# Folding q's second layer into k's in a linear-attention and soft-MoE block on one Trainium2 core

## The reference

```python
def _mlp(x, W1, b1, W2, b2):
    h = jax.nn.gelu(x @ W1 + b1, approximate=False)
    return h @ W2 + b2
q = _mlp(x, W1q, b1q, W2q, b2q)
k = _mlp(x, W1k, b1k, W2k, b2k)
v = _mlp(x, W1v, b1v, W2v, b2v)
scores = jnp.einsum('bid,bjd->bij', q, k) / scale
scores = scores * mask
out = jnp.einsum('bij,bjd->bid', scores, v)
...
x = _layernorm(x + attention, axis=-1)
x = _layernorm(x + soft_moe(x), axis=-1)
```

## Time and profile before

| what | value |
|---|---|
| median of 3 runs | 684.1 us (683.0 to 685.0) |
| the profiled execution: its time, its span | 684.8 us, 683.1 us |
| mean granted TensorE clock | 0.982 |
| PE busy | 643.4 us (94% of the span), 4032 matmuls |
| PEld busy | 581.2 us |
| DVE busy | 446.1 us (65%) |
| ACT busy | 441.2 us (65%) |
| POOL busy | 301.9 us (44%) |

### The profile page before, as it was taken

The page is one execution under the profiler, slowest core; times in us unless marked ns, Lnnn a source line. Parts: engine busy times, 40 slices in busy tenths (PEclk is TensorE's granted clock), DMA queues, the critical chain, the costliest instruction groups (busy, mean ns, idle before and its releaser), DMA issues. The chain is left out here.

```text
span 683.1 us, 12110 instructions
## 1 busy us (share of the span) xinstructions
PE 643.4 (94%) x4032; PEld 581.2 (85%) x4032; DVE 446.1 (65%) x912; ACT 441.2 (65%) x910; POOL 301.9 (44%) x325
## 2 busy tenths in 40 slices
PE   5899999999999999999999999965999999979994
PEld 4789899888898998998988989955999999967883
DVE  5457677677677775776767767776555555345884
ACT  4655767767767668677677676645666666524775
POOL 2433654745536447446365374324433333202443
PEclk9989999999999999999999999996999999999998
DMA  7201201112102011020120100003000000030444
GB/s 240 62 32 32 61 5 60 32 32 62 31 31 61 11 50 34 28 61 31 31 61 31 31 32 1 1 0 63 0 1 0 0 0 1 1 62 31 155 154 154
DMA packets 29299, 30.19 MB, mean 44 GB/s; under 512 B 5298, under 2 KB 25172, under 8 KB 29268
## 3 DMA queue, kind: packets, MB, share of 16 engines
q1 hardware_dynamic: 29248, 29.78, 14.4%
q10 hardware_dynamic: 20, 0.01, 0.0%
HBM read 21.39 MB, written 8.39 MB: 44 GB/s over the span
## 5 line engine op out<-in xcount | busy, mean ns | idle before, releaser
L419 POOL TENSOR_TENSOR v_lo<-xn_all,v_hi 128x512 fp32r<-128x512 f32 x32 | 41.3, 1291 | 114.1 <-ACT v_hi L494 114.1
L476 ACT ACTIVATE h_hi<-bank,bias_col 128x512 fp32r<-128x512 f32 x96 | 66.3, 691 | 31.1 <-PE bank L580 29.0
L856 DVE TENSOR_TENSOR state_lo<-bank,state_hi 128x512 fp32r<-128x512 f32 x58 | 40.0, 690 | 61.6 <-ACT state_hi L509 61.6
L578 PE MATMUL bank<-xnT_hi,w_hi 128*128 128x512 f32 x192 | 77.3, 403 | 1.6 <-DVE xnT_lo L810 1.6
L579 PE MATMUL bank<-xnT_lo,w_hi 128*128 128x512 f32 x192 | 77.2, 402 | 0.0
L580 PE MATMUL bank<-xnT_hi,w_lo 128*128 128x512 f32 x192 | 77.0, 401 | 0.0
L1256 PE MATMUL bank<-xn_all,e_tok 128*128 128x257 f32 x256 | 66.4, 382 | 0.1
L816 DVE TENSOR_TENSOR h_lo<-bank,h_hi 128x512 fp32r<-128x512 f32 x64 | 44.1, 689 | 34.1 <-ACT bank L478 34.1
L1167 ACT ACTIVATE e_tok<-bank,shift,xinv 128x256 f32<-128x256 f32 x64 | 36.1, 564 | 42.6 <-PE bank L1241 21.8
L1336 DVE COPY ET_all<-bank 128x256 f32 (+1 forms) x64 | 27.1, 424 | 55.1 <-PE bank L1250 54.9
L413 POOL TENSOR_TENSOR h_lo<-xn_all,h_hi 128x512 fp32r<-128x512 f32 x32 | 41.4, 1294 | 35.6 <-ACT xn_all L478 33.8
(11 more groups left out here) (168 smaller groups left out, 2118.3 us busy)
## 6 DMA issues: line engine op xcount, KB each, us to landing
xn_all<-in_xT SPq DMA_DIRECT2D x16, 512.0 KB, 3.7
x_all<-in_L_attn_x SPq DMA_DIRECT2D x16, 512.0 KB, 3.5
out<-xn_all SPq DMA_DIRECT2D x16, 512.0 KB, 3.0
w_sb<-in_L_ffn_w SPq DMA_DIRECT2D x2, 512.0 KB, 5.2
xn_all<-in_L_ffn_w SPq DMA_DIRECT2D x2, 512.0 KB, 6.4
x_all<-in_L_attn_W1k SPq DMA_DIRECT2D x1, 256.0 KB, 4.2
x_all<-in_L_attn_W1q SPq DMA_DIRECT2D x1, 256.0 KB, 4.6
x_all<-in_L_attn_W1v SPq DMA_DIRECT2D x1, 256.0 KB, 4.8
```

Source lines behind the costliest of these rows:

```text
L419: pool.tensor_tensor(v_lo[:, pair, :], v_tok[:, pair, :], v_hi[:, pair, :].bitcast(F32), ALU.subtract).then_inc(v_split, 1)
L476: nc.scalar.activation(h_hi[:, n, m, :], ps, ACT.Gelu, bias=bias(n, m))
L578: nc.tensor.matmul(ps, w[0], xs[0], start=start, stop=False, skip_group_check=shared)
L856: nc.vector.tensor_tensor(lo[:, :, :], state_halves, hi[:, :, :].bitcast(F32), ALU.subtract).then_inc(state_split, 1)
```

## The change

The product q . k is rewritten. With hq and hk the gelu outputs, q = hq W2q + b2q and k = hk W2k + b2k, so q . k = hq . (W2q k) + b2q . k. The kernel therefore computes once M = W2k W2q^T (`fold_weights`, 258 columns: 256 of the product and two equal ones, W2k b2q) and for each tile k' = hk M + a constant row (`project_k`, token-major, 128x258). q's second layer is gone; scores and state use hq itself. Column 256 of k' is gamma_j = b2q . k_j, one number per key. It enters the scores as a number added before the mask (`mask_scores`, now four operations, one for each chunk), and for all earlier chunks as the running sum of gamma_j v_j, which is the same row for all later queries: `carry` adds gamma times v of this chunk, with gamma's column as a broadcast weight, to the output tile of the next chunk, and ACT's `preload` copies that tile on to the one after. The scores of a group move from the end of its own body to the next body, behind the first hidden job; all four chunks come later in a body. k' is now in token-major form at first, so k's rounding for the state reads SBUF and its subtraction moves from DVE to POOL (`split_ktok`), and the transposed copy goes through ACT and DVE (`round_kT`, `split_kT`). Six column loads of b2q and b2k (128 elements of 4 bytes each) are new.

```diff
-            HK, HQ, HV, K2, Q2, V2, KT = (0, 1), (2, 3), (4, 5), (6, 7), (8, 9), (10, 13), (11, 12)
...
+            HK, HQ, HV, K2, V2, KT = (0, 1), (2, 3), (4, 5), (6, 7, 8, 9), (10, 12), (11, 13)
...
                     a = g - 1
                     if project:
                         add_ln_b(g)
+                        split_hv(g, 0)
                     if attend:
                         invert_o(a, 0)
                     if project:
-                        split_hv(g, 0)
                         split_hv(g, 1)
                         if more:
                             split_x(g + 1)
+                        split_ktok(g, 0)
                     if attend:
                         invert_o(a, 1)
                     if project:
+                        split_ktok(g, 1)
...
+                for kb in range(KB):
+                    for col in (D, D + 1):
+                        act.dma_start(w2q_in[:, kb, col:col + 1], b2q[kb * P:(kb + 1) * P].rearrange(
+                            "(p o) -> p o", o=1)).then_inc(fold_loaded, 16)
...
+                def round_ktok(g):
+
+                    if not (isinstance(g, int) and g == 0):
+                        act.wait_ge(chunk_done, GT * g)
+                    act.wait_ge(k_biased, GT * g + GT)
+                    nc.scalar.copy(gam_hi[:, :], k_tok[:, :, D]).then_inc(gam_rounded, 1)
+                    for m in range(2):
+                        pair = slice(2 * m, 2 * m + 2)
+                        nc.scalar.copy(ktok_hi[:, pair, :], k_tok[:, pair, 0:D]).then_inc(ktok_rounded, 1)
+
+                def round_kT(g, j, m):
+                    act.wait_ge(kT_done, KB * g + m + 1)
+                    nc.scalar.copy(k_hi[:, m, :], job_bank(j, KT[m])[:, :]).then_inc(kT_rounded, 1)
+
+                def preload(ba, i):
+
+                    act.wait_ge(carried, CB * ba + i - 1)
+                    act.wait_ge(z_ready, TB * ba + i + 2 - i % 2)
+                    nc.scalar.copy(out_tile(i % GT), out_tile((i - 1) % GT)).then_inc(preloaded, 1)
...
+                    def follow(c):
+                        i = GT * ja + c
+                        if i + 1 < TB:
+                            round_state(ba, i + 1)
+                        if i + 2 < TB:
+                            preload(ba, i + 2)
+
...
-                        round_state(ba, GT * ja + 3)
-                    round_k(g, j, 0)
-                    round_k(g, j, 1)
-                    if attend and ja < GB - 1:
-                        round_state(ba, GT * ja + 4)
-                    round_q(g, j, 0)
-                    round_q(g, j, 1)
+                        follow(2)
+                        if settle:
+                            apply_z(act, a - 1, (ja - 1) % 2, range(GT))
+                        follow(3)
+                    round_ktok(g)
+                    round_kT(g, j, 0)
                     round_v(g, 0)
-                    round_ktok(g, j, 0)
-                    if attend and settle:
-                        apply_z(act, a - 1, (ja - 1) % 2, (1, 2, 3))
...
+                def fold_weights():
+
+                    pe.wait_ge(fold_loaded, 16 * 8)
+                    for half in range(KB):
+                        for kb in range(KB):
+                            last = nc.tensor.matmul(out_ps[half][:, 0:KC], w2k_in[:, kb, half * P:(half + 1) * P],
+                                                    w2q_in[:, kb, :], start=(kb == 0), stop=(kb == KB - 1))
+                    last.then_inc(m_done, 1)
...
+                def mark_out():
+
+                    pe.wait_ge(m_split, KB)
+                    for ps in out_ps:
+                        last = nc.tensor.matmul(ps[:, :], ident[:, :], causal[:, :, :].rearrange("p c n -> p (c n)"),
+                                                start=True, stop=True)
...
+                def project_k(g, j, t):
+                    if t < 2:
+                        pe.wait_ge(hkq_split, 4 * g + t + 3)
+                    else:
...
+                        last = split3(job_bank(j, K2[t])[:, 0:KC], (h_hi[:, K_SLOT, kb, toks], h_lo[:, K_SLOT, kb, toks]),
+                                      (m_hi[:, kb, :], m_lo[:, kb, :]), kb == 0, kb == KB - 1)
+                    last.then_inc(k_done, 1)
...
+                def carry(a, ba, i):
+
+                    c = i % GT
+                    if c == 0:
+                        pe.wait_ge(gam_split, a + 1)
+                    if i > 0:
+                        pe.wait_ge(preloaded, PB * ba + i)
+                    split3(out_tile((i + 1) % GT),
+                           (gam_hi[:, c:c + 1].to_broadcast([P, P]), gam_lo[:, c:c + 1].to_broadcast([P, P])),
+                           (v_hi[:, c, :], v_lo[:, c, :]), False, False, shared=True).then_inc(carried, 1)
+
+                def chunk(a, ja, ba, c, p):
                     i = GT * ja + c
-                    if c % 2 == 0:
-                        pe.wait_ge(z_ready, GT * a + c + 2)
+                    if 0 < i < TB - 1:
+                        pe.wait_ge(preloaded, PB * ba + i)
                     if i == 0:
+                        pe.wait_ge(z_ready, GT * a + 2)
                         last = attend_chunk(a, c, True, True)
                     elif c == 0:
-                        read_state(ba, i, c, True, False)
+                        read_state(ba, i, c, p, False)
                         last = attend_chunk(a, c, False, True)
                     else:
-                        attend_chunk(a, c, True, False)
-                        last = read_state(ba, i, c, False, True)
+                        attend_chunk(a, c, False, False)
+                        last = read_state(ba, i, c, p, True)
                     last.then_inc(chunk_done, 1)
                     if i < TB - 1:
                         update_state(a, c, i == 0)
...
+                        carry(a, ba, i)
...
                     a, ja = g - 1, (j - 1) % GB
+                    p = q_slot(j - 1)
                     if not project:
-                        last_chunks(a, ja, ba)
+                        last_chunks(a, ja, ba, p)
                         return
-                    if attend:
-                        chunk(a, ja, ba, 0)
-                    else:
+                    if not attend:
                         turn_biases()
                     hidden(g, j, WK1, 0)
+                    if attend:
+                        scores(a, p, range(GT))
                     hidden(g, j, WK1, 1)
+                    if not attend:
+                        fold_weights()
                     hidden(g, j, WQ1, 0)
                     if attend:
-                        chunk(a, ja, ba, 1)
+                        chunk(a, ja, ba, 0, p)
                     hidden(g, j, WQ1, 1)
                     hidden(g, j, WV1, 0)
+                    if attend:
+                        chunk(a, ja, ba, 1, p)
                     hidden(g, j, WV1, 1)
-                    if attend:
-                        chunk(a, ja, ba, 2)
-                    project_kq(g, j, WK2, 0)
-                    project_kq(g, j, WK2, 1)
-                    if attend:
-                        chunk(a, ja, ba, 3)
-                    project_kq(g, j, WQ2, 0)
-                    project_kq(g, j, WQ2, 1)
+                    project_k(g, j, 0)
+                    project_k(g, j, 1)
+                    if attend:
+                        chunk(a, ja, ba, 2, p)
+                    project_k(g, j, 2)
+                    project_k(g, j, 3)
+                    if attend:
+                        chunk(a, ja, ba, 3, p)
                     project_v(g, j, 0)
                     turn_k(g, j, 0)
-                    scores(g)
+                    project_v(g, j, 1)
                     turn_k(g, j, 1)
-                    project_v(g, j, 1)
                     if not attend:
+                        mark_out()
                         sum_mu_squares()
...
+                def bias_k(g, j, t):
+                    dve.wait_ge(k_done, GT * g + t + 1)
+                    if isinstance(g, int) and g == 0:
+                        dve.wait_ge(ku_ready, 1)
+                    nc.vector.tensor_tensor(k_tok[:, t, :], job_bank(j, K2[t])[:, 0:KC], ku_rows[:, :], ALU.add
+                                            ).then_inc(k_biased, 1)
+
+                def split_gamma(g):
+                    dve.wait_ge(gam_rounded, g + 1)
+                    nc.vector.tensor_tensor(gam_lo[:, :], k_tok[:, :, D], gam_hi[:, :].bitcast(F32), ALU.subtract
...
+                def mask_scores(a):
+                    dve.wait_ge(scores_done, a + 1)
+                    for c in range(GT):
+                        last = nc.vector.scalar_tensor_tensor(out=masked[:, c, :], in0=masked[:, c, :],
+                                                              scalar=k_tok[:, c, D:D + 1], in1=causal[:, c, :],
+                                                              op0=ALU.add, op1=ALU.mult)
```

(43 more changed lines are left out.)

326 lines of the change are left out of this document (187 added, 139 removed).

## The result

The changed kernel took 711.4 us in the median of four runs (703.2 to 716.8), the kernel before 684.5 beside it. The ratio is 1.030, with a 95% interval of 1.025 to 1.036. It is slower, as forecast, but the time lies above my 696 us and outside the range of 680 to 703. The profiled execution took 706.8, with a span of, by chance, also 705.0 us.

A forecast was written before the change was run, and what follows sets the result against it. PE was taken to bound the steady attention stage. The terms -41.8 + 21.6 + 29.2 + 2.0 + 1.5 = +12.5 us on the profiled 684.8 gave 697.3, or 696 against the median, with a range of 680 to 703.

The forecast's parts named there:

- PE's work: PE in the steady attention stage: 26.2 us of work per ordinary group after the change.
- The saving of 2.61 us: PE per group: 24 matmuls of 258 columns replace 24 of 512, 41.8 us less over 16 groups.
- the carries: New PE matmuls behind each chunk but a batch's last: 60 x 0.36 = 21.6 us more.
- The late `k_lo`: PE at the scores waits for DVE's last split_kT, ending at U + 7.5: 2.2 us per ordinary group, 29.2 in all.
- a lock of `ve_o`: On DVE, `ve_o` is held until POOL's split of k' ends, at U + 3.15 (U: end of chunk 3's state update).
- The covers: Mask, state between chunks 2 and 3, and preloads are hidden behind PE's other work: cost nothing.
- The start: Program start: six column loads, `fold_weights` and `mark_out` cost +2.0 us, from 0 to 5.
- the sum's silent term of zero for the clock: TensorE's clock behind PE's new waits: the sum held no cost for it, so waits counted only their length.
- the end: Attention stage's tail: PE waits for the last split_kT, with last scores and mask there: +1.5 us, from 0 to 4.
- The second: Rival: no lock on the path, DVE's queue alone holds PE 1.3 us in ordinary groups: 683 us, chance 0.20.
- The third: Rival: the last split_kT comes in time and PE keeps its 20.2 us: 667 us, chance 0.12.
- The fourth: Rival: broadcast-weight or 258-column matmuls cost more, or TensorE's clock falls at the stalls: 705 to 720 us, chance 0.08.

The follow-up runs named there:

- idle time filled: Changed kernel with useless 512-column matmuls on PE during the waits for the last k_lo, 8 before long waits, 3 before short ones: 687.9 us.
- PE's order: Changed kernel with the scores one hidden job later, behind both K jobs, and chunk 0 behind both Q jobs: 671.6 us, ratio 0.980 to the kernel before.
- without the lock: Changed kernel with POOL's first split of k' behind its second inverse root and gamma's subtraction behind the last split of k^T: 682.7 us, ratio 0.999.
- longer wait: Changed kernel with one more 0.6 us DVE operation ahead of the last split of k^T in each group: 732.6 us.
- before, with idle time: Kernel before, with four 0.6 us DVE operations ahead of the split of the masked scores in 12 groups: 723.2 us.
- DVE's new order: Changed kernel with DVE splitting both halves of k^T before it drains the last pair of chunks: 666.0 us, ratio 0.973 to the kernel before.
- both orders: Changed kernel with k^T split before DVE's drain and the scores behind both K jobs on PE: 661.1 us, ratio 0.968 to the kernel before.

## Why the prediction was right in the wait and wrong in what the wait costs

**Right.** PE's work: 26.22 us. The saving of 2.61 us and the carries at 0.35 us: both have starts 0.12 us apart. The late `k_lo`, through DVE's queue behind the drain, with a lock of `ve_o` on POOL's split of k': its end was U + 7.2 (forecast 7.5), the wait 1.92 us (2.2), and the period without a fall 28.22 us (28.4). The covers: between 60 and 440 us PE waits for neither `masked_lo` nor `state_lo` nor the preload. The start: PE reaches the first hidden job of body 1 at 32.46 us, where the kernel before starts that body at 35.45; that is 2.99 less, with 2.61 saved and 2.70 of scores moved out. In the kernel before, the clock was already down ahead of that point: its eight one-column matmuls and the step to body 1 took 2.12 us (33.33 to 35.45), in the changed kernel, at full speed, 1.30 (31.16 to 32.46). These 0.82 us have nothing to do with the edits, so the edits cost 3.1 us (forecast 2.0). The row of the changed kernel:

```profile
31.16 1.05 PE L844 MATMUL bank<-ones,mu_unit 128*128 128x1 f32 x8
```

**The step that failed** is the sum's silent term of zero for the clock: a wait of PE was priced at its own length alone, and the falls of the clock behind such waits, which the sum left out, cost 16.0 us net. I had put the fall behind the stalls among the rivals at 0.08, because the clock stayed up behind an idle time of 1.60 us and fell behind one of 2.68. Two rows are no bracket: they were one draw each from something that isn't decided by the length alone. And I had missed a third restart in the same trace, behind 2.16 us, the very length that I forecast for the new waits. Behind it the clock fell within 1.5 us, in PE's timeline and windows of the kernel before:

```profile
458.46 0.36 PE L578 MATMUL bank<-h_hi,q_hi 128*128 128x256 f32 x1 [2.16 <-DVE h_lo L856]
```

```profile
459.00:460.00 1.00, 0.81 (x8) 0.97 0.00 0
460.00:461.00 1.00, 1.00 (x6) 0.50 0.00 0
```

With eleven such waits ahead, it should have made the fall a term of the sum. What the runs showed, one profiled execution each, by the idle time ahead of the scores in the profile (in the kernel before with idle time, ahead of chunk 0):

| idle time | kernel | falls behind it |
|---|---|---|
| none (filled) | idle time filled | 0 of 14 |
| to 0.4 us | PE's order | 0 of 11 |
| 0.76 us | changed; without the lock | 0 of 3; 1 of 3 |
| 1.04 us | without the lock | 1 of 11 |
| 1.36 us | longer wait | 3 of 3 |
| 1.75 us | changed | 7 of 11 |
| 1.8 to 2.6 us | before, with idle time | 9 of 12 |
| 2.3 us | longer wait | 10 of 11 |

**The account.** For the spans, +21.9 us (705.0 against 683.1): PE's saving in bodies 1 to 15 -39.2; their 57 carries +20.0; waits 11 x 1.90 + 3 x 0.92 = +23.7 (forecast 29.2); falls 5 x 3.2 + 2 x 1.6 = +19.2, less one fall of 3.2 that only the kernel before has, behind its start, of which 0.8 are in the start already, so -2.4; the start -3.0; the end, from the last of PE's work in body 15 to the first logits, 27.0 instead of 23.6 us, +3.4; the rest of the program -0.4. That makes 21.3, and 0.6 are unexplained. In the start and the end 2.7 us of scores only change places; without them and its three carries the end is 0.4 us shorter than before, where I had put +1.5. So my error of 9.5 us on the profiled execution has a part that I lacked, +16.0 for the clock, and parts that went the other way, above all the waits, -5.5. Without the clock the profiled execution would have taken some 691 us; that of the filled version, which also has no fall behind its start, took 690.9. This is the account of the profiled execution, the only one with a trace.

In the waits the ordinary ones were over-priced by 0.3 each, and the three behind a batch's end by 0.7: there `ve_o` and gamma both slipped through ahead of POOL, where I had gamma caught. At the end the last `k_lo` was late by 1.5 us more than the last bias of v before, as forecast, and a fall behind that wait costs PE about 1.7 more. Against that, the waits of 0.37, 0.78 and 0.77 us that PE had there before are gone.

**The rivals.** The second (no lock) would have come out near the 683 that I gave it: the version without the lock took 682.7. That it hits so closely is partly luck, since its two short falls (3.2 us) are as much as the one fall that only the kernel before has. The third (the stall below 1.3 us, and the change turns to gain) is what DVE's new order makes: 666.0, where I had 667. The fourth happened beside the first, not in its place. It should have been a term with a price per stall and a chance per stall.

## What to carry to other kernels

An engine that was never idle hides what idle time costs. When a change opens a recurring wait of even 1 us on PE, price it twice: the wait, and a chance of a fall of the clock (here 1.6 to 4.8 us each), and treat one or two restarts in the trace as single draws. Look for the wait first where the order of a side engine's queue puts a drain nobody waits for ahead of an operand that PE waits for; moving four operations on DVE turned a loss of 3% into a gain of 2.7%. If a wait can't be removed, filling it with useless matmuls is a cheap test of how much of the loss is the clock, and sometimes part of a cure.

## What the runs showed of the hardware

- TensorE's clock fell to half behind waits of PE as short as 0.76 us (once in six), in an engine that was otherwise without a gap, and not behind one of 2.56 us. At the changed kernel's scores the fall began 0.5 to 2.5 us after PE had begun again; with the longer wait, from 0.3 us before that to 2.8 behind it.
- The four executions of the changed kernel have spans of 701.5, 705.0, 714.1 and 715.0 us and mean granted clocks of 0.962, 0.958, 0.945 and 0.945. The time that the lower clock costs, estimated as the span times the clock's shortfall, is 27 us in the first and 39 in the last, and grows nearly as much as the span. Only the second has a trace, so whether the others differ by falls behind the same waits is not shown. The versions without long waits at the scores spread as well, up to 6 us (both orders, 660.3 to 666.2, clock 0.989 and 0.982).
- Weights that are one column broadcast, and 258 columns instead of 256, cost PE nothing that the timeline shows: their matmuls start 0.12 us apart (228.55 and 228.67; 23.63 and 23.75 us), like the others of 256 columns.
